# A gated feed-forward kernel: the buffers and queue order of the turned h, and eight product groups split over 64 tokens

## Chip, core and metric

The kernel runs on one core of one Trainium2 chip. The metric is the device time of one execution in microseconds (us); the time before is 306.36 us, the median of 2 runs (305.8 and 306.92).

## The reference, cut to what matters

There are 2048 tokens of 512 features (x is 4 x 512 x 512).

```
x = x + tanh(g_xattn) * experts(layernorm(x))
    # 4 experts, chosen by token id; each: g = silu(h W^T), u = h W^T, y = (g*u) W, all with the same 512 x 512 ctx_2048[e]
x = x + tanh(g_ffn) * ffn(layernorm(x))
    # ffn: gate = silu(bit_linear(h, gate_w)), val = bit_linear(h, val_w), bit_linear(gate * val, out_w)
    # bit_linear: x rounded to 8-bit steps by its row's maximum, w rounded to -1, 0, 1 by the mean of abs(w); 2048 hidden columns
```

## The kernel before, in words

Everything is written out by hand, engine by engine, with semaphores between the engines. SyncE (SP) issues the plain loads and the transposes by DMA, one after the other in program order; a wait on SP holds everything behind it. GpSimd (POOL) issues the gathers and scatters and rounds weights.

Stage 1, the experts. Tokens are sorted by expert into 19 units of 128 tokens (`UNITS`). For unit j, TensorE computes a(j) = h times the expert's weights (12 matmuls of 128 x 128 by 512 columns: h and the weights are each split in a high and a low fp16 half, three passes of four, `product`, L619 to L640), ScalarE takes the silu and VectorE the product `gu` (L1155). TensorE turns gu (`turn_gu`, L645) and computes y(j), 12 matmuls more. The order on TensorE (`slot`, L657) is: turn_gu(j-1), a(j), and then y(j-1). Its accumulators lie in PSUM (`banks`).

The product needs h turned, features on the partitions. For units 0 to 8 TensorE turns it (L613). For units 9 to 18 (`H_DMA`), VectorE's norm (L1129) leaves h in a PSUM bank, ScalarE writes the high fp16 half (L867) and VectorE the low one (`h_low`, L1151, counted by `hTlo_made`), and SP turns both at once with a DMA transpose (`turn_h` of `block.sync`, L277 to L281) into one of two buffers `hT_dma`, picked by j % 2. The product waits for the landing (L668 and L669). From unit 11 on, turn_h(j) waits at L280 until a(j-2) is done (`a_done` at j-1), since that product reads the buffer's old contents. On VectorE the order in slot j is, among others: norm(j+2), the statistics of unit j+3 (L1136, which wait for its gather), gu(j), h_low(j+2), x1(j-1) (L1168). So h_low(j) stands behind gu(j-2), which waits for silu(j-2), which waits for a(j-2).

In between, SP loads the FFN weights, 12 pieces of 1024 KB (`load_weights(n)`, L283 to L290, four each of gate, val and out), into `raw`. Pieces 0 to 8 are issued ahead of the first turn_h; so is piece 9, after a wait for the gather of unit 10 (L323). Pieces 10 and 11 follow turn_h(9) and turn_h(11). ScalarE sums their absolute values (`sum_abs`, L895; two per piece, in slots that the table `SUMMED` names: piece 9 in slot 11, piece 10 in slot 12, piece 11 in slot 13, each first sum ahead of that slot's silu, L880), POOL rounds them and ScalarE takes the sign into `tern`.

Stage 2, the FFN, in 16 tiles of 128 tokens. SP turns the rounded tile (`turn_x`, L306) into `xiT`. `ffn_slot(t)` (L764) computes gate and val (`gate`, `val`, L719 and L728) for two chunks c of 1024 hidden columns: each call is 2 banks x 4 contractions = 8 matmuls, 128 tokens stationary (one weight load each) and 512 columns of `tern` moving. Then come 16 matmuls per tile of the output product (`down`, L740), three tiles behind. Tiles 1 and 2 have no `down` between their gates and vals. VectorE empties the accumulators with a scale and a bias (L1245 for gate, L1253 for val), POOL multiplies gate and val (L496), VectorE takes the maximum (L1260). `ring` holds three pairs of banks, so a gate or val call waits for VectorE to have emptied the pair it writes (`v_made`, `g_made`).

Of the kernel before, what the change touches and what calls it, by code (L numbers as in the profile page):

```python
# [5 lines left out]
def gated_block(nc, x, token_ids, ctx_w, g_xattn, g_ffn, gate_w, gate_b, val_w, val_b, out_w, out_b, out):  # L6
    f32, f16, bf16 = mybir.dt.float32, mybir.dt.float16, mybir.dt.bfloat16
# [3 lines left out]
    P = 128  # L11
# [3 lines left out]
    KD = D // P  # L15
# [5 lines left out]
    HC = H // D  # L21
    G = H // P
# [15 lines left out]
    ROUNDED = (0, 0, 0, 0, 0, 0, 2, 4, 6, 8, 8, 9, 10, 12, 14, 16, 20, 24, 24, 24, 24)  # L38
    SIGNED = (0, 0, 0, 0, 0, 0, 0, 1, 3, 5, 7, 8, 9, 10, 12, 14, 16, 17, 18)
    EARLY_SLOT = 15  # L40
    H_DMA = range(9, 19)
    WARM = 30
    HOT = (0, 8, COLS)
    COPIED = (1, 2, 4, 3, 5, 6)
# [10 lines left out]
    with ctx:  # L55
        def sb(name, shape, dt):
            return ctx.enter_context(nc.sbuf_tensor(name, shape, dt))

        def sem(name):
            return ctx.enter_context(nc.semaphore(name))  # L60
# [4 lines left out]
        tern = sb("tern", [P, 3 * G, D], bf16)  # L65
# [9 lines left out]
        def h16_of(j):  # L75
            return h16[(j - H_DMA[0]) % 2]

        def h_of(j):
            return h_next if isinstance(j, int) and j == H_DMA[-1] + 1 else h_sb[:, :]
        gu_sb = sb("gu_sb", [P, D], f32)  # L80
        turned = sb("turned", [P, 4, D], f16)
        hTs = [(turned[:, 0, :], turned[:, 1, :]), tuple(tern[:, 2 * G + i, :].bitcast(f16) for i in (4, 5))]
        hT_dma = tern[:, 2 * G + 6:2 * G + 10, :].bitcast(f16).rearrange("p (b i) d -> p b i d", b=2)
        guT_hi, guT_lo = turned[:, 2, :], turned[:, 3, :]
        x1_sb = sb("x1_sb", [P, XS, ROW], f32)
        ident32 = sb("ident32", [P, P], f32)
# [69 lines left out]
        xiT = area(D, bf16).rearrange("p (b k m) -> p b k m", b=2, m=P)  # L156
# [29 lines left out]

        def hT_of(j):
            if isinstance(j, int) and j in H_DMA:
                return tuple(hT_dma[:, j % 2, i, :] for i in range(2))
            return hTs[isinstance(j, int) and j == 1]  # L190

        w_pair = [banks[:, 4:6, :], banks[:, 2:4, :], banks[:, 6:8, :], banks[:, 4:6, :],
# [1 line left out]
        ring = [banks[:, 6:8, :], banks[:, 0:2, :], banks[:, 2:4, :]]  # L194
# [31 lines left out]
        a_done, silu_made, gu_made = sem("a_done"), sem("silu_made"), sem("gu_made")  # L226
# [20 lines left out]
        def h_turn_of(j):  # L247
            return h_turned[(j - H_DMA[0]) % 2], 16

        def h_turned_to(j):  # L250
            return h_turned[(j - H_DMA[0]) % 2], 16 * ((j - H_DMA[0]) // 2 + 1)

        block = ctx.enter_context(nc.Block(no_gpsimd_drain=True))

        def flat(ap):
            return ap.rearrange("p a b -> p (a b)")
# [3 lines left out]
        def _(sp):  # L260
# [13 lines left out]
            def gathers_landed(j):  # L274
                sp.wait_ge(gathered[j % XG], 16 * (j // XG + 1))

            def turn_h(j):  # L277
                sp.wait_ge(hTlo_made, j + 1)
                if j >= H_DMA[0] + 2:
                    sp.wait_ge(a_done, j - 1)  # L280
                sp.dma_start_transpose(hT_dma[:, j % 2, :, :].rearrange("p i (k m) -> p (i k) m", m=P), h16_of(j)).then_inc(*h_turn_of(j))  # L281

            def load_weights(n):  # L283
                m, q = n // 4, n % 4
                if n == 8:
                    sp.wait_ge(whi_made, PIECES)
                    sp.wait_ge(w_copied, LOW_DVE)
                    sp.wait_ge(wlo_pool, PIECES - LOW_DVE)
                w = (gate_w, val_w, out_w)[m]
                sp.dma_start(flat(raw[:, m * G + 4 * q:m * G + 4 * q + 4, :]), w[:, q * H:(q + 1) * H]).then_inc(raw_loaded[n], 16)  # L290
# [29 lines left out]
                gathers_landed(n + 2)  # L320
                load_weights(n)
            load_weights(8)
            gathers_landed(10)  # L323
            load_weights(9)

            for i, j in enumerate(H_DMA[:-4]):
                turn_h(j)
                if i in (0, 2):
                    load_weights(10 + i // 2)
            sp.wait_ge(signed, x_frees)  # L330
            stored_units(EARLY)
            sp.wait_ge(low_scattered, 16 * len(BOTH))
            load_rows(0)
            load_rows(1)
            turn_h(H_DMA[-4])
            load_rows(2)
            load_rows(3)
            turn_h(H_DMA[-3])
            for t in range(4, EARLY):
                load_rows(t)  # L340
# [243 lines left out]
        def _(pe):  # L584
# [5 lines left out]
            for s in range(1, COLS + 1):  # L590
                last = nc.tensor.matmul(prefix_ps[:, s * E:], ones16[:, :], mask_flat[:, 0:(COLS + 1 - s) * E],
                                        start=False, stop=(s == COLS))
# [3 lines left out]
            for c in range(COLS):  # L596
                if c in HOT:
                    pe.wait_ge(hot_made, HOT.index(c) + 1)
                last = nc.tensor.matmul(perm_ps, row_hot[:, :, c], unit_hot[:, c, :],
                                        start=(c == 0), stop=(c == COLS - 1))  # L600
# [56 lines left out]
            def slot(j, before=True, unit=True, after=True, gamma=None, between=None):  # L657
# [3 lines left out]
                if unit:  # L661
                    e4 = expert_of(j)
                    if first:

                        pe.wait_ge(wlo_made, 3)
                    low_made = (hTlo_made, j + 1)
                    if isinstance(j, int) and j in H_DMA:
                        low_made = h_turned_to(j)  # L668
                        pe.wait_ge(*low_made)  # L669
                    elif isinstance(j, int) and j == 0:  # L670
                        pe.wait_ge(hThi_half, 1)
                    else:
                        pe.wait_ge(hThi_made, j + 1)
                    product(a_of(j), *hT_of(j), e4, low_made,
                            j + 1 if isinstance(j, int) and j < E else None, between).then_inc(a_done, 1)
# [13 lines left out]
            for half, made, done in ((0, h_half, hT_half), (1, h_made, hT_done)):  # L689
                pe.wait_ge(made, 1)  # L690
                for k in range(KD // 2):
                    last = nc.tensor.transpose(first_hT[half][:, k * P:(k + 1) * P],
                                               h_of(0)[:, (half * KD // 2 + k) * P:(half * KD // 2 + k + 1) * P], ident32[:, :])
# [16 lines left out]
            slot(UNITS - 1, after=False)  # L710


            def gate(t, n, c, pair, start=False):

                if not start:
                    pe.wait_ge(v_made, n - 1)
                for b in range(2):
                    for k in range(KD):
                        last = nc.tensor.matmul(ring[pair][:, b, :], flat(xiT[:, bass.ds(t % 2, 1), k, :]),  # L719
                                                tern[:, k * HC + 2 * c + b, :], start=(k == 0), stop=(k == KD - 1))  # L720
                last.then_inc(g_done, 1)

            def val(t, n, c, pair, start=False):
                if not start:
                    pe.wait_ge(g_made, n)
                for b in range(2):
                    for k in range(KD):
                        last = nc.tensor.matmul(ring[pair][:, b, :], flat(xiT[:, bass.ds(t % 2, 1), k, :]),  # L728
                                                tern[:, G + k * HC + 2 * c + b, :], start=(k == 0), stop=(k == KD - 1))
                last.then_inc(v_done, 1)  # L730

            def down(t, half, start=False, to=o_ps):
# [44 lines left out]
            pe.wait_ge(x_turned, 16)  # L777
            pe.wait_ge(signed, G)
            gate(0, 0, 0, 0, start=True)
            val(0, 0, 0, 1, start=True)  # L780
            e4 = expert_of(UNITS - 1)
            pe.wait_ge(guThi_made, UNITS)
# [19 lines left out]
            t = TILES - 3  # L802
# [3 lines left out]
            t = TILES - 2  # L806
# [621 lines left out]
```

## Time and profile before

| what | value |
|---|---|
| median of 2 runs | 306.36 us (305.8 to 306.92) |
| profiled execution, its own time | 307.64 us |
| span of its profile | 305.9 us |
| mean granted TensorE clock | 0.993 of full speed |
| TensorE busy | 291.0 us, 95% of the span |
| VectorE busy | 256.2 us, 84% |
| ScalarE busy | 225.1 us, 74% |
| GpSimd busy | 235.1 us, 77% |

Times in the profile are microseconds from the span's start, for one execution. PE is TensorE's matmuls, PEld its weight loads, DVE VectorE, ACT ScalarE, POOL GpSimd, SPq SyncE's queue. A matmul's own duration is longer than the distance to the next, since they are pipelined.

### The profile page before, as it was taken

How to read it: one execution, taken by the hardware profiler on the slowest of the kernel's cores; microseconds unless marked ns; L12 is line 12 of the kernel's file. 1: busy time of each engine (PE TensorE's matmuls, PEld its weight loads, DVE VectorE, ACT ScalarE, POOL GpSimd, SP SyncE). 2: the span in 40 equal slices, each digit the busy share in tenths (PEclk: the TensorE clock that was granted, in tenths of full speed). 3: DMA queues.
4: the chain of work that ended last, by engine and by line, in shares of the span. 5: the costliest groups of instructions: out<-in, count | busy, mean ns of one | idle time of the engine just before them, and what ended most of it. 6: DMA issues, size and time to landing. Idle time of an engine off the chain costs nothing.

```text
span 305.9 us, 5312 instructions
## 1 busy us (share of the span) xinstructions
PE 291.0 (95%) x1424; PEld 141.0 (46%) x1439; DVE 256.2 (84%) x422; ACT 225.1 (74%) x311; POOL 235.1 (77%) x258
## 2 busy tenths in 40 slices
PE   1999999997999999999999999999999999999994
PEld 1445555553554554444444444444444444444453
DVE  5789978886789886799999899998898889887972
ACT  6959686785887855678997797777966886776650
POOL 3546864788688887967777899999889887977862
PEclk9999999997999999999999999999999999999999
DMA  6888688789796999512253644865444433543142
GB/s 239 290 285 321 234 272 303 265 255 314 213 183 158 241 260 340 145 53 53 78 112 60 123 86 104 133 143 105 108 114 104 95 70 78 118 89 86 50 103 106
DMA packets 60998, 49.63 MB, mean 162 GB/s; under 512 B 53231, under 2 KB 53231, under 8 KB 58672
## 3 DMA queue, kind: packets, MB, share of 16 engines
q1 hardware_dynamic: 56416, 35.96, 46.2%
q0 software_dynamic: 4560, 13.40, 13.0%
q8 instruction: 11, 0.18, 0.3%
q14 instruction: 11, 0.09, 0.1%
HBM read 28.35 MB, written 10.00 MB: 125 GB/s over the span
## 4 chain that ended last, share of the span: by engine, by line
PE 77%; DMA 8%; DVE 6%; ACT 3%; issue 2%; POOL 2%; SPq 1%; DVEq 0%; POOLq 0%
PE banks L638 23%; PE banks L719 17%; PE banks L740 17%; PE banks L728 16%; DMA raw<-in_ctx 3%; DMA tern<-tern 2%; PE banks L645 2%; DMA raw<-x_low 2%; DMA xg<-in_x,gather_at 1%; PE banks L759 1%; DVE raw L1245 1%; DVE raw L1260 1%; SPq L300 1%; PE banks L613 1%; ACT tern L901 1%
## 5 line engine op out<-in xcount | busy, mean ns | idle before, releaser
L496 POOL TENSOR_TENSOR w_both<-raw 128x1024 f32<-128x1024 f32 (+1 forms) x32 | 75.1, 2346 | 6.1 <-DVE raw L1253 4.2
L638 PE MATMUL banks<-w_both,turned 128*128 x324 | 74.4, 379 | 0.9 <-ACT turned L884 0.8
L728 PE MATMUL banks<-tern,raw 128*128 128x512 bf16 x255 | 60.3, 379 | 0.4 <-DVE raw L1245 0.3
L969 ACT ACTIVATE w_both<-w_both,magic,raw 128x1024 f32 (+1 forms) x31 | 38.2, 1234 | 29.8 <-DVE raw L1270 29.8
L719 PE MATMUL banks<-tern,raw 128*128 128x512 bf16 x251 | 59.9, 379 | 0.3
L740 PE MATMUL banks<-tern,xg 128*128 128x512 bf16 x232 | 55.6, 379 | 0.7 <-DVE raw L1278 0.3
L638 PEld LDWEIGHTS banks<-w_both,turned 128*128 128x128 f16 x324 | 31.7, 98 | 36.0 <-issue 2.7
L1245 DVE SCALAR_TENSOR_TENSOR raw<-banks,raw 128x1024 f32<-128x1024 f32 x32 | 41.0, 1281 | 8.0 <-issue 7.2
L1253 DVE SCALAR_TENSOR_TENSOR raw<-banks,raw 128x1024 f32<-128x1024 f32 x32 | 40.9, 1277 | 3.5 <-PE banks L728 3.5
L1260 DVE TENSOR_REDUCE raw<-w_both 128x1 f32<-128x1024 f32 (+1 forms) x32 | 38.7, 1211 | 3.1 <-POOL w_both L496 2.7
L728 PEld LDWEIGHTS banks<-tern,raw 128*128 (+1 forms) x256 | 24.7, 98 | 31.3 <-DVE raw L1245 2.0
L719 PEld LDWEIGHTS banks<-tern,raw 128*128 (+1 forms) x256 | 25.0, 98 | 30.0 <-DMA raw<-raw 0.3
L994 ACT ACTIVATE raw<-raw 128x1024 f32<-128x1024 f32 x32 | 33.4, 1045 | 6.1 <-DVE raw L1245 6.1
L740 PEld LDWEIGHTS banks<-tern,xg 128*128 (+1 forms) x240 | 23.4, 98 | 28.6 <-issue 0.8
L638 PE MATMUL banks<-w_both,tern 128*128 x132 | 32.1, 394 | 1.8 <-DMA tern<-tern 1.8
L541 POOL TENSOR_SCALAR w_both<-w_both,magic,one 128x1024 bf16<-128x1024 f32 x15 | 18.0, 1198 | 13.8 <-ACT w_both L969 13.3
L491 POOL TENSOR_SCALAR raw<-raw,inv_gam,magic 128x1024 f32<-128x1024 f32 x24 | 28.5, 1190 | 0.0
L399 POOL DMA_INDIRECT xg<-in_x,gather_at x19 | 20.3, 1070 | 10.3 <-DVE gather_at L1103 5.6
L901 ACT ACTIVATE tern<-raw,magic 128x1024 bf16<-128x1024 f32 x24 | 26.7, 1142 | 0.0
L895 ACT ACTIVATE tern<-raw 128x1024 bf16<-128x1024 f32 x24 | 25.3, 1055 | 0.3
L880 ACT ACTIVATE gu_sb<-banks 128x512 f32<-128x512 f32 x19 | 11.3, 596 | 18.9 <-PE banks L638 18.9
L556 POOL DMA_INDIRECT out<-raw x16 | 16.9, 1055 | 8.1 <-DVE raw L1278 3.6
(137 smaller groups left out, 417.9 us busy)
## 6 DMA issues: line engine op xcount, KB each, us to landing
raw<-in_ctx SPq DMA_DIRECT2D x4, 1024.0 KB, 7.5
raw<-in_L_ffn_gate_w SPq DMA_DIRECT2D x4, 1024.0 KB, 5.6
raw<-in_L_ffn_val_w SPq DMA_DIRECT2D x4, 1024.0 KB, 5.2
raw<-in_L_ffn_out_w SPq DMA_DIRECT2D x4, 1024.0 KB, 8.1
raw<-x_low SPq DMA_DIRECT2D x8, 257.5 KB, 4.5
raw<-x_high SPq DMA_DIRECT2D x8, 257.5 KB, 3.2
raw<-in_L_ffn_gate_b SPq DMA_DIRECT2D x1, 1024.0 KB, 6.2
raw<-in_L_ffn_val_b SPq DMA_DIRECT2D x1, 1024.0 KB, 8.1
```

The lines of the kernel that those rows point to most:

```text
L491: nc.gpsimd.tensor_scalar(w, w, inv_gam[:, m:m + 1], magic[:, 0:1], ALU.mult, ALU.add).then_inc(rounded, 1)
L496: nc.gpsimd.tensor_tensor(z[:, t % 2, 2 * D * c:2 * D * c + width], g_sb[:, c, 0:width], v_sb[:, c, 0:width], ALU.mult).then_inc(z_made, 1)
L638: last = nc.tensor.matmul(acc[:, :], a[:, k * P:(k + 1) * P], flat(w[:, bass.ds(e4 + k, 1), :]), start=(k == 0 and i == 0), stop=(k == KD ...
L719: last = nc.tensor.matmul(ring[pair][:, b, :], flat(xiT[:, bass.ds(t % 2, 1), k, :]), tern[:, k * HC + 2 * c + b, :], start=(k == 0), stop ...
L728: last = nc.tensor.matmul(ring[pair][:, b, :], flat(xiT[:, bass.ds(t % 2, 1), k, :]), tern[:, G + k * HC + 2 * c + b, :], start=(k == 0), ...
L740: last = nc.tensor.matmul(to, flat(ziT[:, bass.ds(t % 2, 1), k, :]), tern[:, 2 * G + k, :], start=(k == 0), stop=(k == G - 1))
L901: nc.scalar.activation(flat(tern[:, bass.ds(2 * p, 2), :]), flat(raw[:, bass.ds(2 * p, 2), :]), ACT.Sign, bias=magic[:, 1:2]).then_inc(sig ...
L969: nc.scalar.activation(zq[:, a:b], flat(z[:, bass.ds(t % 2, 1), a:b]), ACT.Identity, scale=flat(sc[:, bass.ds(t, 1), 12:13]), bias=magic[: ...
L994: nc.scalar.activation(g_sb[:, c, :], g_sb[:, c, :], ACT.Silu).then_inc(s_made, 1)
L1245: v.scalar_tensor_tensor(g_sb[:, c, :], flat(ring[(4 * t + 2 * c + 1) % 3 if t else 0]), col(t, 3), bias_g[:, 2 * c * D:2 * (c + 1) * D], ...
L1253: v.scalar_tensor_tensor(v_sb[:, c, :], flat(ring[(4 * t + 2 * c + 2) % 3 if t else 1]), col(t, 4), bias_v[:, 2 * c * D:2 * (c + 1) * D], ...
L1260: v.tensor_reduce(col(t, 5 + c), z[:, t % 2, 2 * D * c:2 * D * (c + 1) + c], AX.X, ALU.max, apply_absolute_value=True).then_inc(zmax_made, 1)
```

## The change

Three things. The turned h gets three buffers in place of two (`HT`), and turn_h(j) waits for a(j-3) in place of a(j-2). Weight pieces 9, 10 and 11 are issued behind turn_h(9), turn_h(11) and turn_h(13), and the wait for the gather of unit 10 ahead of piece 9 is dropped. In tiles 1 and 2, each matmul of gate and val becomes two: tokens 0 to 63 stationary into partitions 0 to 63 of the bank, then tokens 64 to 127 into partitions 64 to 127, both with the same 512 moving columns.

```diff
-    H_DMA = range(9, 19)
+    H_DMA, HT = range(9, 19), 3
...
-        hT_dma = tern[:, 2 * G + 6:2 * G + 10, :].bitcast(f16).rearrange("p (b i) d -> p b i d", b=2)
+        hT_dma = tern[:, 2 * G + 6:2 * G + 12, :].bitcast(f16).rearrange("p (b i) d -> p b i d", b=HT)
...
-                return tuple(hT_dma[:, j % 2, i, :] for i in range(2))
+                return tuple(hT_dma[:, j % HT, i, :] for i in range(2))
...
             def turn_h(j):
                 sp.wait_ge(hTlo_made, j + 1)
-                if j >= H_DMA[0] + 2:
-                    sp.wait_ge(a_done, j - 1)
-                sp.dma_start_transpose(hT_dma[:, j % 2, :, :].rearrange("p i (k m) -> p (i k) m", m=P), h16_of(j)).then_inc(*h_turn_of(j))
+                if j >= H_DMA[0] + HT:
+                    sp.wait_ge(a_done, j - HT + 1)
+                sp.dma_start_transpose(hT_dma[:, j % HT, :, :].rearrange("p i (k m) -> p (i k) m", m=P), h16_of(j)).then_inc(*h_turn_of(j))
...
             load_weights(8)
-            gathers_landed(10)
-            load_weights(9)
 
             for i, j in enumerate(H_DMA[:-4]):
                 turn_h(j)
-                if i in (0, 2):
-                    load_weights(10 + i // 2)
+                if i in (0, 2, 4):
+                    load_weights(9 + i // 2)
...
+            def in_parts(t):
+                return isinstance(t, int) and 1 <= t <= 2
+
+            def parts(t):
+                return (slice(0, P // 2), slice(P // 2, P)) if in_parts(t) else (slice(0, P),)
+
             def gate(t, n, c, pair, start=False):
...
                 for b in range(2):
                     for k in range(KD):
-                        last = nc.tensor.matmul(ring[pair][:, b, :], flat(xiT[:, bass.ds(t % 2, 1), k, :]),
-                                                tern[:, k * HC + 2 * c + b, :], start=(k == 0), stop=(k == KD - 1))
+                        for r in parts(t):
+                            last = nc.tensor.matmul(ring[pair][r, b, :], xiT[:, t % 2, k, r] if in_parts(t) else flat(xiT[:, bass.ds(t % 2, 1), k, :]),
+                                                    tern[:, k * HC + 2 * c + b, :], start=(k == 0), stop=(k == KD - 1))
                 last.then_inc(g_done, 1)
```

The loop in `val` is changed in the same way.

## Rows read from the trace of the kernel before

**Rows 1.** The page: busy share of the span and instructions of each engine.

```profile
PE 291.0 (95%) x1424; PEld 141.0 (46%) x1439; DVE 256.2 (84%) x422; ACT 225.1 (74%) x311; POOL 235.1 (77%) x258
```

**Rows 2.** The chain in order of time: start us, length us, what.

```profile
72.55 7.04 PE banks L638 x24
...
85.78 5.18 PE banks L638 x24
...
158.79 1.73 PE banks L740 x8
...
298.36 3.51 PE banks L759 x32
```

**Rows 3.** Timeline of PE around unit 9: start us, length us, [idle before].

```profile
72.55 4.45 PE L638 MATMUL banks<-w_both,tern 128*128 x12 [1.82 <-DMA tern<-tern]
...
79.86 2.75 PE L638 MATMUL banks<-w_both,tern 128*128 x12
```

**Rows 4.** 72.6 to 76 us: length; PE, PEld, DVE, ACT, POOL busy; granted clock; DMA share; GB/s.

```profile
72.60:76.00 3.40, 3.40 (x10) 1.36 (x11) 1.06 (x3) 0.08 (x1) 3.01 (x3) 0.58 0.99 377
```

**Rows 5.** Timeline of SyncE's queue: issues of pieces 9 to 11 and turns 9 to 13.

```profile
63.23 0.33 SPq L290 DMA_DIRECT2D raw<-in_L_ffn_out_w  x1
65.71 1.65 SPq L281 DMA_TRANSPOSE tern<-tern  x1
67.41 0.73 SPq L290 DMA_DIRECT2D raw<-in_L_ffn_out_w  x1
70.64 1.23 SPq L281 DMA_TRANSPOSE tern<-h_sb  x1
78.98 1.23 SPq L281 DMA_TRANSPOSE tern<-tern  x1
80.26 0.58 SPq L290 DMA_DIRECT2D raw<-in_L_ffn_out_w  x1
84.60 1.23 SPq L281 DMA_TRANSPOSE tern<-h_sb  x1
90.35 1.23 SPq L281 DMA_TRANSPOSE tern<-tern  x1
```

**Rows 6.** DMA issues from 63 to 64 us: the last figure is us to landing.

```profile
raw<-in_L_ffn_out_w SPq DMA_DIRECT2D x1, 1024.0 KB, 8.4
```

**Rows 7.** DMA issues from 67.3 to 68 us: a weight piece, and the transpose still being issued.

```profile
raw<-in_L_ffn_out_w SPq DMA_DIRECT2D x1, 1024.0 KB, 8.5
tern<-tern SPq DMA_TRANSPOSE x1, 6.7
```

**Rows 8.** DMA issues, 70 to 72, 80 to 81 and 84 to 85 us.

```profile
tern<-h_sb SPq DMA_TRANSPOSE x1, 6.5
...
raw<-in_L_ffn_out_w SPq DMA_DIRECT2D x1, 1024.0 KB, 5.3
tern<-tern SPq DMA_TRANSPOSE x1, 3.0
...
tern<-h_sb SPq DMA_TRANSPOSE x1, 5.3
```

**Rows 9.** Line L280, SyncE's wait for the product: count, duration ns, first and last start.

```profile
L280 SPq EVENT_SEMAPHORE  x8: 17/17/17, 77.0 to 116.6; - x8
```

**Rows 10.** Timeline of VectorE: the statistics of unit 12 and the wait for its gather.

```profile
75.72 0.69 DVE L1136 BATCH_NORM_STATS2 bn<-xg 128x6 f32<-128x512 f32 x1 [2.34 <-DMA xg<-in_x,gather_at]
```

**Rows 11.** Timeline of ScalarE: first sum of piece 11 and the silu behind it.

```profile
97.55 1.06 ACT L895 ACTIVATE tern<-raw 128x1024 bf16<-128x1024 f32 x1
...
99.64 0.60 ACT L880 ACTIVATE gu_sb<-banks 128x512 f32<-128x512 f32 x1 [0.94 <-PE banks L638]
```

**Rows 12.** Stretches of tiles 1 and 2 and after, columns as in rows 4.

```profile
140.60:154.60 14.00, 13.84 (x64) 6.00 (x63) 13.90 (x17) 12.67 (x15) 9.39 (x6) 1.00 0.28 76
154.60:165.00 10.40, 10.01 (x47) 4.30 (x47) 9.60 (x14) 9.30 (x13) 8.72 (x6) 1.00 0.60 113
```

**Rows 13.** Timeline of PE: tiny matmuls with a weight load each.

```profile
3.65 0.71 PE L591 MATMUL banks<-mask,ones 128*128 128x64 bf16 x16
```

More of the change, by code:

```diff
@@ L727, in val @@
                     for k in range(KD):
-                        last = nc.tensor.matmul(ring[pair][:, b, :], flat(xiT[:, bass.ds(t % 2, 1), k, :]),
-                                                tern[:, G + k * HC + 2 * c + b, :], start=(k == 0), stop=(k == KD - 1))
+                        for r in parts(t):
+                            last = nc.tensor.matmul(ring[pair][r, b, :], xiT[:, t % 2, k, r] if in_parts(t) else flat(xiT[:, bass.ds(t % 2, 1), k, :]),
+                                                    tern[:, G + k * HC + 2 * c + b, :], start=(k == 0), stop=(k == KD - 1))
                 last.then_inc(v_done, 1)
```

## The prediction

> **What bounds the kernel now.** I read the busy shares first, then the chain that ended last in order of time, then PE's waits and timeline around each break in that chain, then SyncE's queue and its landings. PE is busy for 291.0 of 305.9 us [rows 1], and the chain runs on PE's matmuls nearly all the way: 24 matmuls of 512 columns take 5.18 us and 8 take 1.73 [rows 2], so 216 ns each, back to back. An edit pays only if it takes out one of the few breaks or changes what PE itself executes. The largest break is at unit 9, the first whose h is turned by DMA. PE stands idle for 1.82 us until that transpose lands [rows 3], and the matmuls behind the gap run slower: 12 of them spread over 4.45 us where the same 12 later take 2.75 [rows 3]. The granted clock is 0.58 from 72.6 to 76 us [rows 4], most of the time at the lower of its two levels, 1.2 GHz, after the idle stretch and in spite of full work from there on. So the chain has 7.04 us for 24 matmuls that elsewhere take 5.18 [rows 2]. The whole break costs 1.82 + (7.04 - 5.18) = 3.68 us. The other place to look at is tiles 1 and 2 (140.6 to 154.6 us): PE is busy for 13.84 of 14.00 us, and VectorE for 13.90 [rows 12]; the two run level there.
>
> **Pieces 9 to 11 behind the transposes.** turn_h(9) is issued at 65.71, and 2.5 us ahead of it, at 63.23, a 1024 KB piece went out [rows 5] that takes 8.4 us to land [rows 6], so until about 71.6. The transpose lands after 6.7 us [rows 7], at 72.4, shortly behind the piece. With the same queue, turn_h(11), which has no piece just ahead of it, lands in 3.0 us, and turn_h(12), issued 4.3 us behind a piece, in 5.3 [rows 8]. In the changed order turn_h(9) is like turn_h(11): its bounds are 3.0 and 5.3 us, a landing at 68.7 to 71.0, and I take 3.0 to 4.3. PE is ready for it at 72.55 - 1.82 = 70.73. So the wait goes, all of it or all but 0.3 us, and with no idle stretch ahead of it the clock should stay at 2.4 GHz: 3.68 us.
>
> What is late next. turn_h(10), issued at 70.64 [rows 5], is wanted at 79.86 now [rows 3]; with the break gone it is wanted at 79.86 - 3.68 = 76.2, 5.5 us after its issue. It takes 6.5 us now, behind two pieces [rows 7, 8]; in the changed order piece 9 is issued at about 67.4, where piece 10 is now [rows 5], with nothing left of an earlier piece. The nearest row is the 5.3 us of turn_h(12) [rows 8]; at 6.5 us it would stall PE for 1.0. I take 0.3. The gather of unit 12 holds VectorE until 75.72 [rows 10], and gu(9) stands behind it; PE would want gu(9) at 70.73 + 5.18 = 75.9, and gu(9) could be ready two VectorE operations of 0.7 us after the gather. It would stall PE by 1.3 us if that gather landed no sooner than now; but it competes today with the rest of piece 9 and all of piece 10, and in the changed order with one piece alone, so I take that it lands 2 us or more sooner, and cost it at nothing. Piece 9 is wanted by ScalarE two slots later: hidden. Piece 10 goes where piece 11 goes now, behind turn_h(11), and is wanted one slot later than it lands: hidden. Piece 11 is the tight one: behind turn_h(13), issued at 90.35 [rows 5], it goes out at 91.6 and lands 5.3 us later, at 96.9 (or, at 8.5, at 100.1) [rows 7, 8]. Its first sum runs at 97.55, and the silu behind it has 0.94 us of idle ahead [rows 11]. At 5.3 us nothing is late; at 8.5 us the silu is 100.1 - 97.55 - 0.94 = 1.6 us late, and PE loses about 1 of it, since gu(13) has about as much in hand. I take 5.3, the row with the same order of issues. Bounds of this part: a gain of 3.68 us at best, of 3.68 - 1.0 - 1.3 - 1.0 = 0.4 if all three go wrong. I take 3.4.
>
> **Three buffers.** SyncE's wait at L280 looks like a binding one, but it is over at 77.0 for unit 11 [rows 9], while the transpose goes out at 78.98 [rows 5]: h_low(11) comes behind gu(9) in VectorE's order, and gu(9) itself needs a(9). The code has the same order for every unit, so the one wait is contained in the other each of the 8 times. I cost this part at nothing, both ways: the wait that it relaxes is never the last one, and nothing is added.
>
> **The split products.** Two tiles x two chunks x gate and val x 8 = 64 matmuls of 128 tokens become 128 of 64 tokens. Each still streams 512 columns: matmuls of 256 columns take 3.51 / 32 = 110 ns, and of 512 columns 216 [rows 2], so the distance follows the moving columns, and a half of the tokens saves nothing; the lower bound is 0. The upper one is 64 more matmuls of 216 ns, 13.8 us, on PE, which is the bound; of that, PE's idle time there and up to 165 us, 0.16 + 0.39 [rows 12], would cover 0.5 to 0.7. No row of this trace shows two matmuls on different halves of the output partitions. What decides is whether the second half runs while the first does. Issue alone doesn't stop it: 16 tiny matmuls with a weight load each pass in 0.71 us [rows 13], 44 ns per pair of instructions, so two pairs need 90 of the 216 ns. The two halves write different partitions and load different weights, 64 columns each, so together as much weight as now. I take that they run side by side, with 0.2 us left over for starting each second half and for passing from whole to half products and back.
>
> The Trainium skill speaks on both sides here. "TensorEngine Tiling (Array Packing)", Key Properties, says that tiles can load and multiply in parallel and that a change of mode drains the engine; with the 4 ns per further tile of "TensorE: Matmul & The Clock Gate", Part 3 (Measured speedup vs the span model), the estimate for this part would be 0.3 us. The Mechanism section of that same Part 3 says that a weight load overlaps running matmuls only when the row group differs; here both halves use all rows, and by that rule the upper bound would come true. No row here decides between them.
>
> **The sum.** Against the profiled execution's 307.64 us (span 305.9 and 1.7 around it): - 3.4 + 0.2 = 304.4. That execution lies 1.3 us above the median shown, so I carry the difference over: 306.36 - 3.2 = 303.2 us.
>
> **Rivals.**
> - *The halves run one after the other.* PE executes 8 groups of 16 matmuls in place of 8, 3.46 us each in place of 1.73. VectorE is then no limit in tiles 1 and 2. 13.8 - 0.7 - 3.4 = + 9.7 us: 316.1. For it: PE is the bound, and each half streams every column. Against it: separate partitions and weights. It ends on the slower side by 2% from about 147 ns per split matmul on (6.1 + 3.4 = 9.5 us over 64), 0.7 of a matmul.
> - *They overlap in part*, say by half: 6.9 - 0.7 - 3.4 = + 2.8 us, 309.2.
> - *The stall only changes its owner*: turn_h(10), the gather of unit 12 or piece 11 hold PE for 2 us of the 3.4, possibly with the clock falling once more. For it: DMA is busy at a 0.99 share there [rows 4]. 306.36 - 1.4 + 0.2 = 305.2.
> - *The change doesn't do what it says*: that is so of the three buffers, and is in the forecast.
>
> **How the numbers follow.** The forecast, 0.55; the halves in series, 0.20; in part, 0.10; the stall changes its owner, 0.12; something better than I see, 0.03. Two per cent, 6.1 us, is about what a measurement of this kernel can tell from no change; below 300.2 is "faster" and above 312.5 "slower". Faster: 0.03. Slower: the serial case, 0.20. Same: 0.77. The likeliest case's own range is 302.3 (all of 3.68, and a little more) to 305.0. The whole range has to take in the serial case to leave out less than 2 in 10: 302.3 to 316.5.
>
> **What would show it.** Right: the wait of PE on the DMA transpose at unit 9 is gone or below 0.3 us, the granted clock there is 1.00, the chain shows 5.18 us for each 24 matmuls, and what follows up to the FFN starts 3.4 us sooner, with no new wait of ScalarE on piece 11. In tiles 1 and 2, PE has twice the matmuls in the same 14 us, the starts of the halves a few ns apart. SyncE's wait at L280 shrinks, and the turns still go out when h_low ends. Wrong: 27 us for tiles 1 and 2 (serial), or a new wait on the DMA at unit 10, on gu(9), or at the silu of unit 13.

## The result and the profile after

| | before | after | ratio |
|---|---|---|---|
| median of 2 runs | 306.36 us | 311.17 us (310.68 to 311.66) | 1.0152 [1.0103, 1.0201] |
| the same kernel again (e5), 12 runs | 306.6 us | 307.44 us (306.02 to 311.34) | 1.0021 [0.9988, 1.0054] |

Both executions of the first line for the changed kernel have a mean granted clock of 0.994 or less, as have 3 of e5's 12, which took 311.0 to 311.3 us where the other 9 took 306.0 to 309.0; so the second line is nearer to what the change costs, and the ratios, unlike the medians, leave those 3 out. The interval of e5 takes in no change at all, but not the forecast gain of 3.2 us. The profiled execution took 311.66 us (span 309.9).

The page of the changed kernel, busy shares, against [rows 1]:

```profile
PE 291.7 (94%) x1487; PEld 141.6 (46%) x1503; DVE 254.4 (82%) x422; ACT 225.2 (73%) x311; POOL 234.7 (76%) x258
```

There are 63 more recorded matmuls (64 were added), and PE is busy for only 0.7 us more. The time is not in the split matmuls themselves. PE around unit 9 and at its new idle stretches, against [rows 3] (start us, length us, [idle before]):

```profile
70.59 2.76 PE L636 MATMUL banks<-w_both,tern 128*128 x12
...
76.21 2.75 PE L636 MATMUL banks<-w_both,tern 128*128 x12
...
106.09 0.66 PE L643 MATMUL banks<-ident,gu_sb 128*128 128x128 f32 x4 [1.41 <-DVE gu_sb L1161]
...
107.53 4.45 PE L636 MATMUL banks<-w_both,tern 128*128 x12 [0.78 <-DMA tern<-tern]
...
128.29 2.76 PE L636 MATMUL banks<-w_both,tern 128*128 x12 [2.05 <-DMA tern<-h_sb]
```

The break at unit 9 is gone. But what it cost appears again at unit 15: 1.41 + 0.78 us idle, then 4.45 us for 12 matmuls; and 2.05 us idle at unit 18. The same as stretches (columns as in rows 4):

```profile
72.00:78.00 6.00, 6.00 (x32) 2.97 (x30) 5.15 (x11) 5.19 (x9) 5.44 (x8) 1.00 0.67 154
107.50:112.00 4.50, 4.47 (x13) 1.80 (x14) 3.15 (x7) 0.00 (x0) 3.78 (x6) 0.62 1.07 310
143.30:157.40 14.10, 14.10 (x130) 7.00 (x128) 13.68 (x16) 12.30 (x14) 8.89 (x5) 1.00 0.28 75
```

Behind unit 9 the clock is now 1.00 instead of 0.58 [rows 4]; behind the new gap it is 0.62. Tiles 1 and 2 (third line) have 130 matmuls where there were 64 [rows 12], in the same time.

SyncE's queue, against [rows 5], and then the landings of turns 9, 10, 15 and 18 (last figure, us):

```profile
65.62 1.33 SPq L281 DMA_TRANSPOSE tern<-tern  x1
67.00 0.57 SPq L290 DMA_DIRECT2D raw<-in_L_ffn_out_w  x1
70.36 1.25 SPq L281 DMA_TRANSPOSE tern<-h_sb  x1
...
88.63 1.04 SPq L290 DMA_DIRECT2D raw<-in_L_ffn_out_w  x1
...
99.01 1.23 SPq L281 DMA_TRANSPOSE tern<-tern  x1
```

```profile
tern<-tern SPq DMA_TRANSPOSE x1, 3.1
...
tern<-h_sb SPq DMA_TRANSPOSE x1, 4.6
...
tern<-tern SPq DMA_TRANSPOSE x1, 8.4
...
tern<-h_sb SPq DMA_TRANSPOSE x1, 8.6
```

Turn 9 lands in 3.1 us instead of 6.7 [rows 7] and turn 10 in 4.6 instead of 6.5 [rows 8], as forecast. Turns 15 and 18 land late. The chain in order of time says who set the pace between:

```profile
85.48 1.08 POOL xg L397
...
91.57 1.09 POOL xg L397
...
95.58 0.58 POOL rstd L436
96.16 0.03 issue
96.19 0.03 DVE banks L1135
...
99.01 8.39 DMA tern<-tern
107.40 0.13 issue
107.53 7.04 PE banks L636 x24
```

From 65.1 to 96.2 us the chain stays on GpSimd; before, it ran on PE's matmuls from 72.55 to 102.2. GpSimd's gathers, and VectorE's waits, the first two of them on rstd (one over the standard deviation, which GpSimd computes for the norm):

```profile
85.48 1.08 POOL L397 DMA_INDIRECT xg<-in_x,gather_at  x1 [0.18 <-issue]
...
91.57 1.09 POOL L397 DMA_INDIRECT xg<-in_x,gather_at  x1 [0.19 <-issue]
...
97.66 1.09 POOL L397 DMA_INDIRECT xg<-in_x,gather_at  x1 [0.18 <-issue]
```

```profile
90.09 0.81 DVE L1135 TENSOR_SCALAR banks<-xg,mean_var,rstd 128x512 f32<-128x512 f32 x1 [0.58 <-POOL rstd L436]
...
96.19 0.81 DVE L1135 TENSOR_SCALAR banks<-xg,mean_var,rstd 128x512 f32<-128x512 f32 x1 [0.99 <-POOL rstd L436]
...
104.55 0.69 DVE L1142 BATCH_NORM_STATS2 bn<-xg 128x6 f32<-128x512 f32 x1 [2.74 <-DMA xg<-in_x,gather_at]
```

GpSimd's slots are 6.09 us apart (gather, two scatters, one rounding of a weight piece, three small operations), PE's undisturbed slots 5.62 (24 matmuls 5.18 [rows 2], and 0.44 for turning gu in the same chain). From one slot to the next VectorE's wait grows by 0.41 us, near that difference. None of these waits is in the trace of before, whose PE was 3.7 us late from unit 9 on. GpSimd's gathers lay as far apart there:

```profile
87.39 1.08 POOL L399 DMA_INDIRECT xg<-in_x,gather_at  x1 [0.18 <-issue]
...
93.49 1.09 POOL L399 DMA_INDIRECT xg<-in_x,gather_at  x1 [0.19 <-issue]
```

### The profile page after: what moved, and what is told of

It is laid out like the page before. It is cut to its first block, busy times and chain, and to the rows that moved or that the text cites. A ratio compares the mean times of both kernels' runs of the same rounds, so it can differ in the third digit from the quotient of the medians.

```text
span 309.9 us, 5438 instructions
## 1 busy us (share of the span) xinstructions
PE 291.7 (94%) x1487; PEld 141.6 (46%) x1503; DVE 254.4 (82%) x422; ACT 225.2 (73%) x311; POOL 234.7 (76%) x258
## 4 chain that ended last, share of the span: by engine, by line
PE 63%; POOL 11%; DMA 10%; issue 6%; DVE 5%; ACT 3%; SPq 0%; POOLq 0%; DVEq 0%; ACTq 0%
PE banks L636 16%; PE banks L746 16%; PE banks L724 14%; PE banks L734 14%; DMA tern<-h_sb 3%; DMA tern<-tern 3%; DMA raw<-in_ctx 2%; POOL xg L397 2%; POOL x_low L402 2%; POOL w_both L494 2%; DMA xg<-in_x,gather_at 1%; POOL raw L489 1%; PE banks L765 1%; PE banks L643 1%; POOL x_high L402 1%
## 5 line engine op out<-in xcount | busy, mean ns | idle before, releaser
L724 PE MATMUL banks<-tern,raw 128*128 128x512 bf16 (+1 forms) x277 | 59.6, 380 | 1.2 <-DMA raw<-raw 0.6
L734 PE MATMUL banks<-tern,raw 128*128 128x512 bf16 (+1 forms) x285 | 60.2, 380 | 0.4 <-DVE raw L1251 0.2
L724 PEld LDWEIGHTS banks<-tern,raw 128*128 (+2 forms) x288 | 25.3, 100 | 30.7 <-issue 1.5
L734 PEld LDWEIGHTS banks<-tern,raw 128*128 (+2 forms) x288 | 25.1, 100 | 30.7 <-DVE raw L1251 2.0
```

The lines of the kernel that those rows point to most:

```text
L724: last = nc.tensor.matmul(ring[pair][r, b, :], xiT[:, t % 2, k, r] if in_parts(t) else flat(xiT[:, bass.ds(t % 2, 1), k, :]), tern[:, k * ...
L734: last = nc.tensor.matmul(ring[pair][r, b, :], xiT[:, t % 2, k, r] if in_parts(t) else flat(xiT[:, bass.ds(t % 2, 1), k, :]), tern[:, G + ...
```

## The experiments

Times are medians, with the ratio to runs of the kernel before on the same chip. "To the first gate" and "stage 2" (from there to the span's end) are of the profiled execution; before they are 131.41 and 174.49 us, after 134.13 and 175.77. Both of these profiled executions have a stretch at the lower clock in stage 1. The changed kernel's other profile (e5), which has none, shows 130.34 and 175.76: the 1.3 us of stage 2 are there again, the 2.7 us of stage 1 are not.

**The parts alone (e1 to e3).** e1 has the split `gate` and `val` and nothing else, e2 the three buffers (`HT = 3` and its four uses), e3 the queue order:

```diff
 load_weights(8)
-gathers_landed(10)
-load_weights(9)
 for i, j in enumerate(H_DMA[:-4]):
     turn_h(j)
-    if i in (0, 2):
-        load_weights(10 + i // 2)
+    if i in (0, 2, 4):
+        load_weights(9 + i // 2)
```

> The kernel before with nothing but the split products of tiles 1 and 2. Theory (the queue order costs the time, the split is free): within 0.5 us of before, 306.4, tiles 1 and 2 still in 14 us of PE. Rival (the split costs the time, by passing between whole and half products or by holding VectorE): 2 us or more above before.

> The kernel before with nothing but the third buffer for turned h. Theory (its wait is never the last one): within 0.5 us of before, 306.4, the transposes issued at the same times. Rival (the relaxed wait lets a transpose out sooner and into a fuller queue, or changes where it lands): 1 us or more away from before.

> The kernel before with nothing but pieces 9 to 11 behind transposes 9, 11 and 13. Theory: the whole loss is here, 310.5 to 311.5, with the break of unit 9 gone and PE held at units 14, 15 and 18 instead. Rival (the loss needs the third buffer or the split): at most 306.

| run | median (n) | ratio | to the first gate | stage 2 |
|---|---|---|---|---|
| e1 | 307.93 (8) | 1.0053 [1.0019, 1.0088] | 130.13 | 175.87 |
| e2 | 306.13 (10) | 0.9997 [0.9972, 1.0021] | 129.24 | 174.76 |
| e3 | 306.76 (10) | 1.0023 [0.9984, 1.0061] | 129.61 | 174.69 |

The buffers do nothing that can be measured. The loads alone gain nothing; e3's theory, which looked for the whole loss there, missed too. The split alone loses 1.6 us, though its matmuls run as hoped. Of the changed kernel, timeline of PE in tiles 1 and 2:

```profile
143.50 1.92 PE L724 MATMUL banks<-tern,raw 128*64 128x512 bf16 x16
145.25 1.89 PE L734 MATMUL banks<-tern,raw 128*64 128x512 bf16 x16
146.98 1.89 PE L724 MATMUL banks<-tern,raw 128*64 128x512 bf16 x16
148.71 1.89 PE L734 MATMUL banks<-tern,raw 128*64 128x512 bf16 x16
```

16 half matmuls start every 1.73 us, as 8 whole ones do [rows 2]: side by side, with nothing left over that shows. The loss comes later. SyncE's queue (the transposes of the rounded gate times val product, four in a row) and ScalarE in e1:

```profile
152.81 9.45 SPq L314 DMA_TRANSPOSE xg<-w_both  x4
```

```profile
157.42 1.15 ACT L998 ACTIVATE w_both<-w_both,magic 128x1024 bf16<-128x1024 f32 x1 [1.24 <-DMA xg<-w_both]
```

and in e2, where no such wait is:

```profile
151.92 8.24 SPq L314 DMA_TRANSPOSE xg<-w_both  x4
```

In e1 the first of the four lands in 4.5 us, in e2 in 3.1, with the same instructions ahead of it on every engine but PE. ScalarE waits 1.24 us for it, GpSimd for ScalarE, a later tile's `xiT` goes out late, and PE stands idle for 0.47 us on its landing and then for VectorE. One thing lies in that transpose in e1 and not in e2, a packet of the queue that fetches instructions. DMA of e1, 154.5 to 156 us (packets, MB, share of 16 engines):

```profile
q1 hardware_dynamic: 591, 0.15, 141.5%
q8 instruction: 1, 0.02, 4.0%
```

In e2 that packet comes at 167.2 us, in e1 at 154.8. The 128 instructions more that PE executes from tile 1 on (64 matmuls, 64 weight loads) take it forward by about the 14 us that 128 instructions take there. The Trainium skill, "Runtime: NRT & Kernel Launch", Instruction fetch mechanics, says that a sequencer fetches its code through a DMA queue of its own, in blocks of 256 instructions or 16 KiB, and that this is mostly hidden. Size and order of the packets agree (0.02 MB, and PE executes 16 instructions per 1.73 us here, so 256 in 28: in e2 the packets at 138 and 167 us). PE shows no wait of its own there; e6, e9 and e10 ask whether the fetch costs time by way of the transposes.

**Code without split (e6, e9), and half the split (e10).** e6 and e9 leave the products whole and add waits that are long met. e6's 128 waits came to 64 instructions more in the trace, half of what was intended, and missed the first transpose; e9's 320 came to 135. e10 splits tile 1 only (64 more).

```diff
 for k in range(KD):
+    if isinstance(t, int) and 1 <= t <= 2:
+        pe.wait_ge(x_turned, 16)
+        pe.wait_ge(x1_made, UNITS)
```

(e6; e9 has three more such lines.)

```diff
-    return isinstance(t, int) and 1 <= t <= 2
+    return isinstance(t, int) and t == 1
```

(e10, on e1.)

> The kernel before, without the split, with two waits that are already met in front of each of the 64 matmuls of gate and val in tiles 1 and 2: 128 more instructions on TensorE, as many as the split adds, and no other work. Theory (the 128 more instructions move the fetch of TensorE's code from about 167 us to about 154, into the transposes of the first z tile, and that costs the time): the instruction packet lies at 153 to 158 us, that transpose lands about 1.4 us later than before, and the time is 307.5 to 308.5. Rival (the 64-token matmuls themselves cost it): 306 to 306.7.

> The kernel before with five waits that are already met ahead of each of the 64 matmuls of gate and val in tiles 1 and 2, which come to 135 more TensorE instructions (the earlier variant with two waits came to 64, and its code fetch fell at 157.6 us, behind the first z transpose). Theory (the code fetch, moved into the first z transpose, is the split's cost): the fetch packet lies 2 to 3 us behind that transpose's issue, the transpose lands after 4.5 us in place of 3.1, and from the first gate to the end it takes 175.6 to 176.0 us, as with the split, in place of 174.5 to 174.8. Rival (the 64-token matmuls cost it by themselves): 174.5 to 174.8.

> The kernel before with the products of tile 1 alone split, 64 more TensorE instructions. Theory (code fetch): the fetch lies where it did with two waits, some 27.5 us behind the first gate, the first z transpose lands after 3.1 us, and from the first gate to the end it takes 174.5 to 174.9 us. Rival (the 64-token matmuls, or passing between whole and half products, cost it): about 0.6 us or more above that, 175.2 to 175.9.

| run | median (n) | ratio | packet at | late transpose | stage 2 |
|---|---|---|---|---|---|
| e6 | 306.35 (12) | 0.9999 [0.9969, 1.0029] | 157.6 | third, 3.8 us | 174.49 |
| e9 | 308.04 (10) | 1.0029 [1.0000, 1.0058] | 159.2 | second, GpSimd waits 1.32 | 176.05 |
| e10 | 306.96 (10) | 1.0012 [0.9981, 1.0044] | 158.2 | third, 3.7 us | 174.76 |

e9 has no split product and the same loss in stage 2 as e1. GpSimd of e9, and PE behind it:

```profile
161.94 1.20 POOL L541 TENSOR_SCALAR w_both<-w_both,magic,one 128x1024 bf16<-128x1024 f32 x1 [1.32 <-DMA xg<-w_both]
```

```profile
167.29 1.90 PE L725 MATMUL banks<-tern,raw 128*128 128x512 bf16 x8 [0.54 <-DMA raw<-raw]
...
182.16 1.90 PE L752 MATMUL banks<-tern,xg 128*128 128x512 bf16 x8 [0.87 <-DVE raw L1290]
```

e10 has split products and no loss. So it is not the halves. What goes with the loss is where the fetch falls: 1.2 to 2 us behind the issue of the first (the changed kernel, e1, e5) or second (e9) of these transposes, it goes with 1.1 to 1.6 us more of stage 2; in e6 and e10, 0.5 us behind the issue of the third, that one lands 0.6 to 0.7 us later and nothing is lost. The runs with the loss also have twice the added instructions (128 and 135 against 64), so the number and the place are not separated by themselves; the waits of ScalarE and GpSimd on the late transpose speak for the place. In time alone, e9 lies 1.0 ± 1.0 us above e10. What holds the transpose back inside the DMA no run shows.

**The new stalls of stage 1 (e4, e5, e7, e8, e11, e12).** e5 is the changed kernel once more. The others try causes for the late units 15 and 18: e4 puts the pieces behind turns 9, 10 and 11 instead of 9, 11 and 13; e7 (order of before) and e8 (order of e3) load x1's rows behind turns 15 and 16 and the biases behind turn 18; e11 has 128 waits that are met, 64 instructions, ahead of PE's warm-up matmuls, to shift the code fetches in stage 1; e12 is the kernel before with only the biases moved.

```diff
-                if i in (0, 2, 4):
-                    load_weights(9 + i // 2)
+                if i in (0, 1, 2):
+                    load_weights(9 + i)
```

(e4, on the changed kernel.)

```diff
+            turn_h(H_DMA[-4])
             sp.wait_ge(signed, x_frees)
             stored_units(EARLY)
...
             load_rows(0)
             load_rows(1)
-            turn_h(H_DMA[-4])
-            load_rows(2)
-            load_rows(3)
             turn_h(H_DMA[-3])
-            for t in range(4, EARLY):
+            for t in range(2, EARLY):
                 load_rows(t)
             turn_h(H_DMA[-2])
+            turn_h(H_DMA[-1])
             sp.wait_ge(signed, bias_frees)
...
-            turn_h(H_DMA[-1])
```

(e7 and e8; behind `...` stand the three bias loads. e12 moves only `turn_h(H_DMA[-1])` ahead of the wait for `bias_frees`.)

```diff
+            for _ in range(64):
+                pe.wait_ge(consts16, 3)
+                pe.wait_ge(mask_made, 1)
             pe.wait_ge(whi_made, 1)
             keep_warm(WARM)
```

(e11.)

> The changed kernel with pieces 9, 10 and 11 behind transposes 9, 10 and 11, so piece 11 goes out some 11 us sooner. Theory (PE now outruns GpSimd's slots and the late gather and transpose of unit 15 meet each other, not the weights): the loss stays, 309.5 to 311.5. Rival (piece 11 is late for its sums and fills the queue ahead of units 14 and 15): back to 303 to 305, PE not held at units 14 and 15.

> The changed kernel itself, on the chip on which the parts were timed. Theory (the parts add up: +1.6 us for the split, about +0.7 for the order of the loads, 0 for the buffers): 308.0 to 309.5. Rival (the parts interact, and the loss of 4.8 us needs all of them): 310.5 to 311.5.

> The kernel before with SyncE's queue in another order: the eight loads of x1 rows behind transposes 15 and 16, and the three bias loads behind transpose 18. Theory (transposes 15 and 18 land late because row and bias loads go out just ahead of them): both land within 5.5 us, PE is not held at units 15 and 18, 304.5 to 305.5. Rival (they land late through GpSimd's gathers and scatters): 306 or more, transpose 15 still at 6.5 us or more.

> The same with pieces 9 to 11 behind transposes 9, 11 and 13 as well. Theory (the order of the pieces is a gain that the later row and bias loads hide): 303 to 305, no break from unit 9 to 18 above 0.3 us but GpSimd's own slots. Rival (GpSimd's slots of 6.1 us take what is gained): as e7 or slower.

> The kernel before with 128 waits that are already met, 64 more instructions, ahead of TensorE's warm-up matmuls, where it waits for data anyway. In all traces so far the transposes of h that land late are those of units 12, 15 and 18, with a packet of TensorE's code on its way at 83 to 87, 102 to 105 and 120 to 124 us. Theory (the code fetch delays them): the packets come some 5 us sooner, and now units 11, 14 and 17 have the late landings (5.5 us or more) and 15 and 18 land below 5. Rival (gathers, row loads and bias loads delay them): 15 and 18 still land after 5.5 us or more.

> The kernel before with the three bias loads behind the transpose of unit 18. Theory (2.3 MB of biases just ahead of it add to its landing, as its 3.1 us without them showed): unit 18's transpose lands within 5 us, PE is never held there, and the median is 305.7 to 306.4, with no execution above 308. Rival (it is not late often enough to matter): 306.2 to 306.8.

| run | median (n) | ratio | what the profile shows |
|---|---|---|---|
| e4 | 307.37 (11) | 1.0025 [1.0002, 1.0048] | idle 0.46 at unit 15, 2.69 at 18 |
| e5 | 307.44 (12) | 1.0021 [0.9988, 1.0054] | idle 0.36 at 12, 1.87 at 15 |
| e7 | 308.31 (9) | 1.0058 [1.0015, 1.0102] | idle 0.99 at 9; 2.53 in slot 17, GpSimd waits 4.79 for rows |
| e8 | 307.69 (12) | 1.0056 [1.0018, 1.0094] | idle 0.78 at 12, 0.91 at 15, 1.92 in slot 17 |
| e11 | 312.46 (4) | 1.0151 [1.0093, 1.0210] | first product at 23.94 us instead of 17.52 |
| e12 | 306.70 (12) | 0.9992 [0.9964, 1.0020] | turn 18 lands in 4.9 us, nothing gained |

e4, e5, e7 and e8 came out other than their theories said. The rows are not what makes turn 15 late (7.6 us in e8 too), and later rows hold GpSimd and with it, in slot 17, `turned` (the turned gu of unit 16); of e7:

```profile
123.16 2.84 PE L636 MATMUL banks<-w_both,turned 128*128 x12 [2.53 <-ACT turned L882]
```

Early biases do delay turn 18, without a time that can be measured. The place of piece 11 isn't the cause either (e4, where turn 15 lands in 6.5 us and turn 18 in 9.8).

Whether the code fetch is stays open. In the traces of all the other kernels a packet of PE's code lies within the landings of turns 12 and 15, in 15 of these 18 within that of turn 18, and else only within that of turn 9 in the trace of before (6.7 us; e13's turn 9 took as long without one). In e11 the packets lie in turn 11 (4.3 us), just ahead of turn 15 (4.7) and in turn 18 (8.3), while turns 12 and 16 land in 6.1 without one. So the theory that the late landings move along with the packets failed, and a landing of 6.1 us needs none; but turn 15, without a packet, lands sooner than in the other traces of the old order that show its landing (5.2 to 6.8), so a part of its lateness may be the fetch. e11's own loss is another matter: PE's warm-up matmuls start at 14.96 us instead of 8.55, with nothing but the added waits in the 6.23 us ahead of them (the weights that they read were there by 8.5), so 128 met waits are not free in that place.

In all nine profiles with the new order PE has no idle stretch at unit 9, and in nearly all one at unit 12, 15 or 18. In the ten with the old order, before among them, six have one just ahead of unit 9's product, and it is not always the size of [rows 3]: 0.78 in e6, 0.84 in e1, 0.99 in e7, 1.98 in e13, 2.17 in e10, none in e2, e9, e11 and e12. Some of these too have one at unit 15 or 18 (0.80 in e2, 1.88 in e9, 1.44 in e13), so the late landings there are not all the new order's.

e2 is the most telling of them. Its turn 9 landed in 3.2 us without any new order, PE had no break at unit 9, and its chain, too, runs on GpSimd, from 73.9 us on:

```profile
86.16 1.08 POOL xg L399
...
92.25 1.09 POOL xg L399
...
96.26 0.58 POOL rstd L438
...
99.69 6.80 DMA tern<-tern
```

So what brings GpSimd's slots onto the chain is a PE that is not late at unit 9, by whatever cause. It isn't so in every profile: in e3 a late turn 12 (7.6 us) holds PE for 0.77 us, the chain runs over the turns 12, 15 and 18 themselves, and VectorE waits for rstd by 0.28 us at most.

**The tight engine relieved (e13 to e15).** If GpSimd's 6.09 us slots are what takes the gain back, taking one rounding out of slots 11 and 12 each should give it. The tables count, slot by slot, the half pieces that GpSimd has rounded and ScalarE has signed:

```diff
-    ROUNDED = (0, 0, 0, 0, 0, 0, 2, 4, 6, 8, 8, 9, 10, 12, 14, 16, 20, 24, 24, 24, 24)
-    SIGNED = (0, 0, 0, 0, 0, 0, 0, 1, 3, 5, 7, 8, 9, 10, 12, 14, 16, 17, 18)
+    ROUNDED = (0, 0, 0, 0, 0, 0, 2, 4, 6, 8, 8, 8, 8, 10, 13, 16, 20, 24, 24, 24, 24)
+    SIGNED = (0, 0, 0, 0, 0, 0, 0, 1, 3, 5, 7, 8, 8, 8, 10, 13, 16, 17, 18)
```

e13 is that on the kernel before, e14 with the new order of loads, e15 with the biases behind turn 18 as well.

> The kernel before with the roundings of GpSimd's slots 11 and 12 done in slots 14 and 15 (ROUNDED), and ScalarE's signs moved accordingly (SIGNED). Theory (TensorE is held by unit 9's break here, so GpSimd has time in hand): no change, 306 to 306.8. Rival (GpSimd's slots already set the end): 305 or less.

> The same, with pieces 9 to 11 behind transposes 9, 11 and 13. Theory (GpSimd's slots of 6.1 us take the gain of the new order): VectorE no longer waits for the rstd of units 13 and 14, the break at unit 15 is below 0.4 us, the first gate starts at 128.0 to 129.3 us, and the median is 304 to 305.5. Rival (the transposes of units 12, 15 and 18 land late whatever GpSimd does): the breaks stay, first gate at 129.5 or later, 306 to 307.

> The same with the three bias loads behind the transpose of unit 18 as well. Theory: unit 18's transpose lands within 5.5 us, no TensorE break above 0.4 us from unit 9 to 18, median 303.5 to 305, few executions above 307. Rival: as e14, 306 to 307.

| run | median (n) | ratio | to the first gate |
|---|---|---|---|
| e13 | 306.54 (12) | 0.9965 [0.9922, 1.0009] | 132.56 |
| e14 | 305.41 (12) | 0.9927 [0.9889, 0.9964] | 129.70 |
| e15 | 305.06 (12) | 0.9931 [0.9898, 0.9963] | 128.09 |

GpSimd's gathers in e14:

```profile
79.47 1.08 POOL L397 DMA_INDIRECT xg<-in_x,gather_at  x1 [0.19 <-issue]
...
84.36 1.06 POOL L397 DMA_INDIRECT xg<-in_x,gather_at  x1 [0.18 <-POOL x_sb L479]
...
89.24 1.06 POOL L397 DMA_INDIRECT xg<-in_x,gather_at  x1 [0.18 <-issue]
```

They are 4.9 us apart and then 6.1, and VectorE no longer waits for rstd. Turn 15, 8.4 us in the changed kernel, is issued at 99.94 and PE takes it up at 105.95 without a wait, so it landed within 6.0. In e14 to e17 PE is never held at unit 15, in the five profiles with the new order and the old tables always. PE still stands 0.63 us at unit 12 and 0.83 in slot 17. With both, order and tables, the kernel gains 0.7%. What each of them is worth is less clear: e13 (tables alone) has 0.9965 with an interval that takes in 1, e14 lies 0.8 ± 0.9 us below e13 on the same chip, and e14's profiled execution reaches the first gate no sooner than e3's (129.70 and 129.61 us). Against e3, 1.0023 [0.9984, 1.0061], the interval of e14 lies clear, but that is a comparison across two chips. In e15 PE has no idle stretch of 0.3 us or more between unit 9 and the first gate (the one at the gate itself is shown), and none of its 12 executions was over 306.0 us:

```profile
128.09 1.67 PE L717 MATMUL banks<-tern,raw 128*128 128x512 bf16 x7 [0.65 <-DMA raw<-raw]
```

**All of it together (e16, e17).** e16 is the changed kernel with the tables of e13 and the biases behind turn 18. e17 is e15 again, as its partner on one chip: they differ by the split and the buffers.

> The whole change (three buffers, loads behind the transposes, split products) with the roundings moved out of slots 11 and 12 and the bias loads behind the last turned h: the kernel of e15 plus buffers and split. Theory (the parts add: buffers 0, split +1.2 us of stage 2 by the late transpose of z, whatever stage 1 does): 306.3 us, 1.2 above e15, ratio about 0.997; stage 1 without the breaks of units 12 and 15, stage 2 of 175.8 in the profile, and the clock 1.00. Rival (the split's loss needs the disturbed stage 1 of the changed kernel): 305.1, as e15, and a stage 2 of 174.5.

> The kernel of e15 once more, as the partner of e16 on the same chip: the same without split products and with two buffers. Theory: 0.993 of the kernel before, about 305.1 us; stage 1 to the first gate in 128 to 130 us. If the gain of e15 was luck of one chip, the ratio is within 0.3% of 1.

| run | median (n) | ratio | to the first gate | stage 2 |
|---|---|---|---|---|
| e16 | 306.64 (12) | 0.9999 [0.9972, 1.0026] | 128.47 | 176.23 |
| e17 | 305.52 (12) | 0.9966 [0.9940, 0.9992] | 128.68 | 174.52 |

The split (with the buffers) costs 1.1 us here, 1.7 in stage 2, also where stage 1 has only one break (0.84 us at unit 12). The fetch packet lies at 153.0 us in e16, behind the transpose issued at 151.11, whose landing is, in e16 and then in e17:

```profile
xg<-w_both SPq DMA_TRANSPOSE x1, 4.8
```

```profile
xg<-w_both SPq DMA_TRANSPOSE x1, 3.1
```

The gain of the repaired order holds on this chip too, at 0.3% instead of 0.7. That version (order of loads, tables, biases; no split, two buffers) beats the kernel before on both chips, by less than 1%, and the changed one with the same tables (e16).

## Why the prediction failed, step by step

**"Pieces 9 to 11 behind the transposes", - 3.4: wrong, and this decides the result.** Its mechanism was right up to unit 10: turn 9 lands in 3.1 us (3.0 to 4.3 expected), PE's idle stretch and the slow clock there are gone, turn 10 and unit 12's gather delay nobody. Two things failed.
- The size, and this is the step that failed. 3.68 us was read from one execution whose clock had fallen. The other nine profiles with the old order have 0 to 2.2 us idle at unit 9, and the 1.86 us of slower matmuls only one of them (e13). Over all ten that comes to 0.9 us idle and 0.4 of slower matmuls on average, an estimate from different kernels. The median that I carried the difference over to didn't contain this break in full, so there was never 3.4 to win.
- "What is late next" looked at three transfers (turn 10, the gather of unit 12, piece 11) and took each engine's time in hand from the trace of before. That time in hand was the delay itself: with PE sooner at unit 9, new stalls of 0.3 to 2.7 us stand at units 12, 15 and 18 or in slot 17 in the five profiles with the new order and the old tables. One cause, in a part of these profiles, is GpSimd, with 6.09 us per slot against 5.62: it is on the chain of the changed kernel, of e5 and of e2, and with two roundings moved away the stall at unit 15 is gone (e14 to e17). That it is what takes the gain back is not shown to the end: e3 has no gain either, with GpSimd off its chain. The row stood there: gathers 6.1 us apart in the trace of before too. The other cause is that turns 12, 15 and 18 land late (up to 8.6 us in the changed kernel, 9.8 in e4). Why it is these is not settled: rows and piece 11 are excluded for turn 15, the biases for turns 12 and 15, the code fetch for none.

The rival "the stall only changes its owner" (chance 0.12) is what happened, and its remark "possibly with the clock falling once more" too (0.62 in the changed kernel and in e4, 1.00 in e5); but the owner is none of the three that it names. Piece 11 did come late, 6.7 us for 5.3, and ScalarE waited 1.25 us for it at 95.34; e4, where it comes two slots sooner, is no faster, so it wasn't the one that counted.

**"Three buffers", nothing: right within 0.3%.** e2 is 0.9997 [0.9972, 1.0021], and turn_h still goes out when h_low ends.

**"The split products", + 0.2: the mechanism right, the term too small.** The halves run side by side: 16 of them start every 1.73 us, which refutes the two rivals in series or in part. The Trainium skill, "TensorE: Matmul & The Clock Gate", Part 3, The mechanism, says that a weight load overlaps running matmuls only when the row group differs (and allows for the background weight buffer). The traces do not agree with that as the prediction applied it: here both halves use all rows, and their loads overlap. The trace of before already decided it, though the prediction says that no row does: 64 whole matmuls on all rows, with 63 weight loads, pass in 14.00 us, 216 ns each [rows 12]. The Trainium skill, "TensorEngine Tiling (Array Packing)", Key Properties, says that tiles load and multiply in parallel, and the trace agrees, with the same 1.73 us. What the term left out is the instructions as such. With 128 more on PE, its code fetch falls into a DMA transpose that ScalarE waits for; that goes with 1.1 to 1.7 us more of stage 2 and 1.1 to 1.6 more in the time (e1, e16 against e17).

**The sum.** - 3.4 measured as + 0.7 ± 1.2 (e3), 0 as 0, + 0.2 as + 1.6 ± 1.1 (e1): 2.3 us slower than before by the parts, 0.6 ± 1.0 by e5. The two agree within their intervals. That 311.17 us lies in the range to 316.5 is luck: the range reached that far for the serial rival, which isn't what made the kernel slow.

## What to carry to other kernels

Price a stall by several executions, or by another profile of the same kernel, before its removal is counted as a gain: here one profile showed 3.68 us where most of the others had under 1. After taking a delay out of the bounding engine, go through every other engine's slot length against the bound's: one that is slower than the bound can take the gain back, and shifting a piece of its work went with a gain here. And count instructions, not just busy time: an edit free on its own engine can move the code fetch onto a transfer that matters, which some long met waits in the unchanged kernel can show, in a place where they cost nothing themselves.

## What the runs showed of the hardware

- A packet of instruction fetch beside a DMA transpose of 128 x 1024 goes with a landing in 4.5 to 4.8 us instead of 3.1 (e1, e5, e16, the changed kernel), and in 3.7 or 3.8 where it comes 0.5 us behind the issue (e6, e10).
- Two matmuls of 64 columns of weights each, both over all 128 rows, cost together what one of 128 does: 216 ns for both, weight loads included.
- The clock does not follow the idle time alone. In e13, 1.98 us idle is followed by 0.55, in e10 2.17 us by 1.00 and in e7 2.53 us (in slot 17) by 1.00 too (stretches of e13 and e10 behind the gap at unit 9; columns as in rows 4):

```profile
72.30:76.00 3.70, 3.70 (x10) 1.45 (x11) 0.90 (x2) 0.14 (x2) 3.22 (x4) 0.55 1.08 327
```

```profile
73.20:76.20 3.00, 2.76 (x12) 1.17 (x12) 0.52 (x1) 0.17 (x2) 2.82 (x3) 1.00 0.94 379
```

So one trace does not tell what such a gap costs. Where the breaks of stage 1 are few (e14 to e17), none of 48 executions has a mean clock under 0.997; of the 52 of the kernel before on the same two chips, 11 have 0.994 or less.
